# Projections of two tiles in one product: q, k and up from turned norms laid out by chunk, and the first norm two turns ahead

## The chip, the cores and the metric

The kernel runs on one core of one Trainium2 chip. The metric is device time in microseconds (us). The core has TensorE (PE; its weight loads are shown as PEld), VectorE (DVE), ScalarE (ACT), GpSimd (POOL) and SyncE (SP), which here only issues DMAs.

## The reference

The input is x with 8 sequences of 2048 rows of 256 numbers, in fp32. Two residual blocks follow each other:

```python
x = x + _layernorm(_L0_attn_ref(_layernorm(x)))
x = x + _layernorm(_L0_ffn_ref(_layernorm(x)))

# attention: q, k, v = h @ w.T ; sigma = elu + 1
a_mem = sigma_q @ memory                     # over norm = sigma_q @ memory_norm
A = (sq_i @ sk_i.T) * tril                   # chunks of 128 rows, state carried
out = (A @ v_i + sq_i @ S_kv) / den ; S_kv += sk_i.T @ v_i

# ffn: dense part and 1024 gated experts
dense = silu(h @ W_up.T) @ W_down.T          # W_up 1024 x 256
# experts: product keys, top 8 of 8 x 8 sums for each of 4 heads,
#   w = silu((h @ de) * softmax) over the chosen ones, then w @ ue
```

## The kernel before

The 16384 rows are cut into 128 tiles of 128 rows. Tile t belongs to sequence t % 8, so that neighbouring tiles belong to different sequences and the carried state is not in each other's way. Everything is a software pipeline written out by hand: in step s, each engine runs `body`, in which the name `t[k]` is the tile s - k, so the tile that is at stage k. There are 142 steps ("turns" below); each engine runs through its own list in order, and semaphores tie them together. Nothing is reordered by a scheduler: the order of the code is the order of each engine.

The weights stand in SBUF, turned so that a product for a tile has a chunk of weights as stationary operand or as moving operand. Each product over the 256 numbers of a row needs two chunks (`DC` = 2), and each fp32 product is two instructions in the trace. The helper `product` (L691) records nearly all of them.

What TensorE does for a tile, in its order within a turn: up (stage 10: 8 blocks of 128 of W_up, tile as moving operand, 128 columns each, into banks 1 and 2), q and k (stage 7, 4 blocks of 128 columns, into bank 1), v (stage 7), the experts' output `ue,gT` (stage 13), the router `route` (stage 9), sigma_k times sigma_q `sig` (stage 7), half of the experts' input `deT`, the state and memory products (stage 7), the masked product (L817), the second half of `deT`, the addition to the state (L835, stage 8), and the down product `wdownT` (stage 12). PSUM banks 1 and 2 are used by up, by q and k and by the state in turn, so ScalarE has to evict each half of up (`hT`, Silu, L892 and L947) before the next use.

The norms are turned (rows to columns) off TensorE: VectorE makes the norm (`xn1`, `xn2`, L1055), turns it in blocks of 32 x 32 (`xn1_blocks` L1088, `xn2_blocks` L1115), SP writes the blocks to a DRAM buffer (`xn1_way`, `xn2_way`), and reads them back with 8 small DMAs into `xn1T` or `xn2T` (`gather_chunks`, L437: 16 KB each, in pieces of 128 bytes). The experts' weights (`w_blocks` L1127, `w_way`, read back as `g_parts` with 4 DMAs, L430) and sigma_k (`sk_blocks`, `sk_way`, `sk_nat`) go the same way. GpSimd adds up the four heads' weights with two accumulating DMAs per tile, of 1 MB (L597) and of 512 KB (L558), on a queue of its own. All transfers share the core's 16 DMA engines.

First norm: x is loaded in the turn t (`t[0]`), its statistics are made at `t[3]`, the norm at `t[4]`, the turning and the gather at `t[5]`, and q and k are made at `t[7]`. Second norm: norm, turning and gather at `t[8]`, and first use by TensorE at `t[9]`, by `route`, some 10 us into the turn; up follows at `t[10]`. After the step 23 and up to step 120 (`steady`), a few waits that others imply are left out.

## Time and profile before

| | |
|---|---|
| median of 3 runs | 2848.42 us (2846.77 to 2849.49) |
| the profiled execution | 2852.01 us, span 2850.3 us |
| mean granted TensorE clock | 0.997 of full |
| busy: PE, PEld, DVE, ACT, POOL | 99%, 80%, 85%, 89%, 72% |
| chain that ended last | PE 90%, of it L691 84% |
| DMA engines' mean busy share | 7 tenths in most slices |
| GpSimd's queue, SP's queue | 37.6%, 34.2% of 16 engines' span |

The first row is what versions are compared by, the second belongs to the rows shown below. A busy share is the part of the span in which an engine ran an instruction. The chain is the one that ended last, followed back from the end to what released each step.

### The profile page before, as it was taken

How to read it: one execution, taken by the hardware profiler on the slowest of the kernel's cores; microseconds unless marked ns; L12 is line 12 of the kernel's file. 1: busy time of each engine (PE TensorE's matmuls, PEld its weight loads, DVE VectorE, ACT ScalarE, POOL GpSimd, SP SyncE). 2: the span in 40 equal slices, each digit the busy share in tenths (PEclk: the TensorE clock that was granted, in tenths of full speed). 3: DMA queues.
4: the chain of work that ended last, by engine and by line, in shares of the span. 5: the costliest groups of instructions: out<-in, count | busy, mean ns of one | idle time of the engine just before them, and what ended most of it. 6: DMA issues, size and time to landing. Idle time of an engine off the chain costs nothing.

```text
span 2850.3 us, 49057 instructions
## 1 busy us (share of the span) xinstructions
PE 2819.8 (99%) x14724; PEld 2272.4 (80%) x14724; DVE 2422.5 (85%) x6125; ACT 2525.8 (89%) x3618; POOL 2060.4 (72%) x2460
## 2 busy tenths in 40 slices
PE   8899999999999999999999999999999999999999
PEld 6678878878887788788788878887887788788877
DVE  5888888888888888888888888888888888888886
ACT  5898998999899989988998999899988989998997
POOL 3677777777777777777777777777776777777674
PEclk9999999999999999999999999999999999999999
DMA  4677777777777777777777777777777776777664
GB/s 117 140 170 166 167 173 175 162 167 177 171 165 174 168 167 168 171 170 168 169 172 173 165 169 172 170 165 174 173 163 165 175 175 163 169 175 169 153 153 121
DMA packets 592910, 471.71 MB, mean 165 GB/s; under 512 B 377732, under 2 KB 527365, under 8 KB 592645
## 3 DMA queue, kind: packets, MB, share of 16 engines
q0 software_dynamic: 52832, 199.77, 37.6%
q1 hardware_dynamic: 539812, 268.81, 34.2%
q8 instruction: 117, 1.92, 0.3%
q14 instruction: 149, 1.21, 0.1%
HBM read 137.37 MB, written 131.20 MB: 94 GB/s over the span
## 4 chain that ended last, share of the span: by engine, by line
PE 90%; SPq 2%; POOL 2%; ACT 2%; DMA 2%; DVE 1%; issue 1%; POOLq 0%; DVEq 0%; ACTq 0%
PE banks L691 84%; PE banks L835 3%; PE banks L817 2%; SPq L437 1%; SPq L430 1%; POOL sums L539 1%; DMA w_way<-w_blocks 1%; DMA wexp<-wexp 0%; DMA g_parts<-w_way 0%; DVE w_blocks L1127 0%; POOL rstd L525 0%; ACT prob L986 0%; DVE prob L1119 0%; ACT L1008 0%; POOL wexp L597 0%
## 5 line engine op out<-in xcount | busy, mean ns | idle before, releaser
L539 POOL TENSOR_TENSOR sums<-scores 128x1024 f32<-128x1024 f32 x512 | 1005.2, 2047 | 78.2 <-ACT scores L1025 78.2
L525 POOL TENSOR_TENSOR rstd<-var_eps,minus_half 128x1 f32<-128x1 f32 x512 | 508.5, 993 | 42.2 <-ACT y_sq L935 15.6
L691 PE MATMUL banks<-deT,xn2T 128*128 128x512 f32 x1024 | 484.3, 596 | 2.5 <-DVE picked L1074 2.1
L691 PEld LDWEIGHTS banks<-xn2T,wupT 128*128 128x128 f32 x4096 | 477.2, 192 | 9.3 <-DVE state L1181 2.9
L691 PE MATMUL banks<-xn2T,wupT 128*128 128x128 f32 x4096 | 478.2, 275 | 2.1 <-DVE state L1181 2.1
L691 PE MATMUL banks<-ue,gT 128*128 128x256 f32 x2048 | 463.0, 379 | 0.5 <-ACT gT L964 0.5
L691 PE MATMUL banks<-wdownT,hT 128*128 128x256 f32 x2048 | 462.8, 379 | 0.2 <-ACT y_sb L1021 0.2
L691 PEld LDWEIGHTS banks<-wdownT,hT 128*128 128x128 f32 x2048 | 389.0, 190 | 56.9 <-issue 3.0
L691 PEld LDWEIGHTS banks<-ue,gT 128*128 128x128 f32 x2048 | 388.7, 190 | 53.8 <-ACT gT L964 0.9
L577 POOL TENSOR_TENSOR wexp<-wexp,w_last 128x1 f32<-128x1 f32 x127 | 131.8, 1038 | 370.6 <-ACT z_last L1014 370.6
L691 PEld LDWEIGHTS banks<-deT,xn2T 128*128 128x128 f32 x1024 | 185.8, 192 | 135.8 <-issue 125.0
L553 POOL TENSOR_TENSOR cprob<-cmask,cdif 128x112 f32<-128x112 f32 x128 | 58.9, 460 | 273.9 <-DVE cmask L1208 273.9
L691 PE MATMUL banks<-route,xn2T 128*128 128x512 f32 x512 | 240.9, 593 | 1.5 <-ACT xn2T L882 0.8
L1074 DVE SCALAR_TENSOR_TENSOR picked<-sums,cand_best,banks 128x1024 f32<-128x1024 f32 x128 | 163.9, 1280 | 51.5 <-POOL sums L539 51.5
L1173 DVE SCALAR_TENSOR_TENSOR picked<-sums,cand_best,banks 128x1024 f32<-128x1024 f32 x128 | 163.9, 1281 | 47.6 <-PE banks L691 46.8
L1194 DVE SCALAR_TENSOR_TENSOR prob<-picked,rz,prob 128x1024 f32<-128x1024 f32 x128 | 166.2, 1299 | 36.3 <-ACT prob L939 34.2
L1082 DVE SCALAR_TENSOR_TENSOR prob<-picked,rz,prob 128x1024 f32<-128x1024 f32 x128 | 166.7, 1302 | 27.2 <-ACT prob L986 26.8
L947 ACT ACTIVATE hT<-banks 128x512 f32<-128x512 f32 x128 | 76.6, 598 | 125.4 <-PE banks L691 125.1
L1186 DVE SCALAR_TENSOR_TENSOR picked<-sums,cand_best,banks 128x1024 f32<-128x1024 f32 x128 | 163.4, 1276 | 12.8 <-POOL sums L539 12.7
L896 ACT ACTIVATE wexp<-prob 128x1024 f32<-128x1024 f32 x127 | 134.2, 1057 | 39.0 <-DVE w_blocks L1127 38.9
L961 ACT ACT_TABLE_LOAD x128 | 164.2, 1283 | 2.3
L947 ACT ACT_TABLE_LOAD x128 | 164.2, 1283 | 2.3
(162 smaller groups left out, 6658.7 us busy)
## 6 DMA issues: line engine op xcount, KB each, us to landing
wexp<-wexp POOLq DMA_DIRECT2D x127, 1024.0 KB, 9.1
wexp<-wexp POOLq DMA_DIRECT2D x127, 512.0 KB, 4.7
w_way<-w_blocks SPq DMA_DIRECT2D x127, 512.0 KB, 2.7
g_parts<-w_way SPq DMA_DIRECT2D x508, 128.0 KB, 7.5
xn_way<-xn_blocks SPq DMA_DIRECT2D x248, 128.0 KB, 1.8
x_in<-_attn_hidden_states_dram SPq DMA_DIRECT2D x128, 128.0 KB, 2.4
out_dram<-x_out SPq DMA_DIRECT2D x128, 128.0 KB, 1.8
xn1T<-xn_way SPq DMA_DIRECT2D x1000, 16.0 KB, 2.0
```

The lines of the kernel that those rows point to most:

```text
L525: return nc.gpsimd.tensor_tensor(rstd[:, n, m:m + 1], var_eps[:, n, m:m + 1], minus_half[:, :], ALU.pow)
L539: return nc.gpsimd.tensor_tensor(sums[:, k, :, :], scores[:, k, 0:XIN].unsqueeze(2).broadcast_to([P, XIN, NKEYS]), scores[:, HEADS + k, :] ...
L577: nc.gpsimd.tensor_tensor(weights(t[9])[:, 0, LAST_IN:], weights(t[9])[:, 0, LAST_IN:], w_last[:, t[9] % 2:t[9] % 2 + 1], ALU.add).then_in ...
L691: last = nc.tensor.matmul(out, lhs(c), rhs(c), start=(start and c == 0), stop=(stop and c == chunks - 1))
L896: nc.scalar.activation(weights(t[10])[:, 3, :], prob[:, 3, :], ACT.Silu).then_inc(s_head_3_weights_ready, 1)
L947: nc.scalar.activation(flat(hT[:, t[9] % 3, 4:8, :]), u_ps[1][:, :], ACT.Silu).then_inc(s_hidden_1_ready, 1)
L961: nc.scalar.activation(prob[:, 3, :], head(sums, 3), ACT.Exp, bias=neg_max[:, t[9] % 2, 3:4]).then_inc(s_head_3_prob_ready, 1)
L1074: nc.vector.scalar_tensor_tensor(picked[:, 0, :], head(sums, 2), best[:, 2, TOP - 1:TOP], down, ALU.is_ge, ALU.mult).then_inc(s_head_2_sel ...
L1082: nc.vector.scalar_tensor_tensor(prob[:, 2, :], picked[:, 0, :], rz[:, t[10] % 2, 2:3], prob[:, 2, :], ALU.mult, ALU.mult).then_inc(s_head ...
L1173: nc.vector.scalar_tensor_tensor(picked[:, 0, :], head(sums, 0), best[:, 0, TOP - 1:TOP], down, ALU.is_ge, ALU.mult).then_inc(s_head_0_sel ...
L1186: nc.vector.scalar_tensor_tensor(picked[:, 1, :], head(sums, 1), best[:, 1, TOP - 1:TOP], down, ALU.is_ge, ALU.mult).then_inc(s_head_1_sel ...
L1194: nc.vector.scalar_tensor_tensor(prob[:, 1, :], picked[:, 1, :], rz[:, t[9] % 2, 1:2], prob[:, 1, :], ALU.mult, ALU.mult).then_inc(s_head_ ...
```

## The change

Three things change, and one follows from them.

1. `xn1T` and `xn2T` hold four tiles instead of two and are laid out chunk by chunk, so that the same chunk of two neighbouring tiles is one run of 256 columns. From tile 12 on (`PAIRED`) q, k and up are made for two tiles in one product of 256 columns. In even turns of stage 7 k is made for tiles t and t + 1, in odd ones q for t + 1 and t + 2 (q of tiles 12 and 13 is made once extra, in bank 0). Up for the pair is made half in the even tile's turn (blocks 0 to 3), half in the odd one's (blocks 4 to 7), for tiles 12 to 125. `hT` gets a fourth slot and `sig` a third buffer. The last tiles' up stays as it was; the last turn of stage 7 makes neither q nor k.
2. Up in an even turn now reads the second norm of tile u + 1 too, which is at stage 9 in that turn. On SP the gather of `xn2T` moves ahead of `sk_way` and of the read of `g_parts`, right behind `w_way`.
3. q in an odd turn reads the first norm of tile t + 2. So load, statistics, norm and turning of the first norm move: the tiles 10 and 14 (`AHEAD`) are taken along in a turn with another tile, and behind them every tile is one and then two turns ahead (`ahead`). The gather of `xn1T` stands behind the load of x and the gather of `sk_nat`, last in SP's turn but for the store.
4. ScalarE's eviction of up (`hidden`) writes parts of two tiles' `hT`; `sigma` writes two tiles' q or two tiles' k.

```diff
+    PAIRED = 12
+    AHEAD = (10, 14)
+    TURNED = 4
...
-        xn1T = sb("xn1T", [P, 2, DC, P])
-        xn2T = sb("xn2T", [P, 2, DC, P])
+        xn1T = sb("xn1T", [P, DC, TURNED, P])
+        xn2T = sb("xn2T", [P, DC, TURNED, P])
...
-        sig = sb("sig", [P, 2, 2 * DC, P])
+        sig = sb("sig", [P, 3, DC, 2, P])
...
-        hT = sb("hT", [P, 3, IC, P])
+        hT = sb("hT", [P, 4, IC, P])
...
+        def ahead(t, stage):
+            for lead in range(len(AHEAD) + 1):
+                u = t[stage - lead]
+                if u is not None and u not in AHEAD and len([a for a in AHEAD if a < u]) == lead:
+                    return u
+            return None
...
+            def up(t, half):
+                if not paired_up(t):
...
+                else:
+                    first = t // 2 * 2 % TURNED
+                    for k in range(2):
+                        ic = 4 * (t % 2) + 2 * half + k
+                        last = product(two_tiles(u_ps[half])[:, k, :, :], DC, lambda c: wupT[:, c, ic * P:(ic + 1) * P],
+                                       lambda c: xn2T[:, c, first:first + 2, :])
+                return last
+
+            def two_tile_q_or_k(dst, w, t):
+                for ec in range(DC):
+                    last = product(two_tiles(dst)[:, ec, :, :], DC, lambda c: w[:, c, ec * P:(ec + 1) * P],
+                                   lambda c: xn1T[:, c, t % TURNED:t % TURNED + 2, :])
+                return last
...
+                    if paired_up(u) and u % 2 == 0:
+                        moved(pe, s_xn2_blocks_in, u + 1, BLOCKS * DC, LATE, EARLY)
...
+                    elif t[7] % 2 == 0:
+                        two_tile_q_or_k(qk_ps, wkT, t[7]).then_inc(s_qk_in_psum, 1)
+                    elif t[7] < TILES - 1:
+                        two_tile_q_or_k(qk_ps, wqT, t[7] + 1).then_inc(s_qk_in_psum, 1)
...
+                for lead, a in enumerate(AHEAD):
+                    if t[3 - lead] == a:
...
+                        xn1_made(a - 1)
+                        dve.wait_ge(s_xn1_ready, a)
+                    if t[4 - lead] == a:
+                        xn1_turned(a)
```

SP's queue, one steady turn of before, from the store of the output on. `xn_way` stands for both norms' buffers: the first row of it is the second norm's, the next the first norm's.

```order
L483 DMA out_dram<-x_out 128x256
L444 DMA xn_way<-xn_blocks 128x256
L448 DMA xn_way<-xn_blocks 128x256
L452 DMA w_way<-w_blocks 128x1024
L456 DMA sk_way<-sk_blocks 128x256
L430 DMA g_parts<-w_way 32x4x256 x4
L437 DMA xn2T<-xn_way 32x4x32 x8
L437 DMA xn1T<-xn_way 32x4x32 x8
L475 DMA x_in<-in_L_attn_hidden_states_dram 128x256
L430 DMA sk_nat<-sk_way 32x4x64 x4
L483 DMA out_dram<-x_out 128x256
```

The same stretch of the changed kernel:

```order
L535 DMA out_dram<-x_out 128x256
L494 DMA xn_way<-xn_blocks 128x256
L483 DMA xn_way<-xn_blocks 128x256
L502 DMA w_way<-w_blocks 128x1024
L477 DMA xn2T<-xn_way 32x4x32 x8
L511 DMA sk_way<-sk_blocks 128x256
L470 DMA g_parts<-w_way 32x4x256 x4
L520 DMA x_in<-in_L_attn_hidden_states_dram 128x256
L470 DMA sk_nat<-sk_way 32x4x64 x4
L477 DMA xn1T<-xn_way 32x4x32 x8
L535 DMA out_dram<-x_out 128x256
```

The 8 DMAs of `xn2T` now stand in front of `sk_way` and the 4 of `g_parts`; those of `xn1T` stand behind `x_in` and `sk_nat`.

TensorE, one steady turn of before from up on, with what each row waits for:

```order
L691 MATMUL banks<-xn2T,wupT 128x128 [waits state_ready]
L691 MATMUL banks<-xn2T,wupT 128x128 x15
L691 MATMUL banks<-xn1T,wqT 128x128 [waits hidden_1_ready,xn1_blocks_in_1]
L691 MATMUL banks<-xn1T,wqT 128x128 x3
L691 MATMUL banks<-xn1T,wkT 128x128 x4
L691 MATMUL banks<-wvo,xn1T 128x256 x2
L691 MATMUL banks<-ue,gT 128x256 [waits expert_weights_T_ready]
L691 MATMUL banks<-ue,gT 128x256 x7
L691 MATMUL banks<-route,xn2T 128x512 [waits xn2_blocks_in_1]
```

The changed kernel, a turn in which the tile of up is even (q for two tiles):

```order
L747 MATMUL banks<-xn2T,wupT 128x256 [waits hidden_1_ready,state_ready,xn2_blocks_in_1]
L747 MATMUL banks<-xn2T,wupT 128x256 x3
L747 MATMUL banks<-xn2T,wupT 128x256 [waits hidden_0_ready]
L747 MATMUL banks<-xn2T,wupT 128x256 x3
L747 MATMUL banks<-xn1T,wqT 128x256 [waits hidden_1_ready,xn1_blocks_in_1,xn1_blocks_in_0]
L747 MATMUL banks<-xn1T,wqT 128x256 x3
L747 MATMUL banks<-wvo,xn1T 128x256 x2
L747 MATMUL banks<-ue,gT 128x256 [waits expert_weights_T_ready]
L747 MATMUL banks<-ue,gT 128x256 x7
```

And the turn ahead of it, with an odd tile at up (k for two tiles):

```order
L747 MATMUL banks<-xn2T,wupT 128x256 [waits hidden_1_ready,state_ready]
L747 MATMUL banks<-xn2T,wupT 128x256 x3
L747 MATMUL banks<-xn2T,wupT 128x256 [waits hidden_0_ready]
L747 MATMUL banks<-xn2T,wupT 128x256 x3
L747 MATMUL banks<-xn1T,wkT 128x256 [waits hidden_1_ready]
L747 MATMUL banks<-xn1T,wkT 128x256 x3
```

In place of 16 products of 128 columns for up and 8 for q and k stand 8 and 4 of 256 columns. In the even turn the very first product of up waits for `xn2_blocks_in_1`, the gather of tile u + 1's second norm, for which `route` waits too, but later in the same turn; the first product of an odd turn waits for no gather.

## Rows read from the trace of the kernel before

**Rows 1.** The page, part 1: busy time and share of the span of each engine.

```profile
PE 2819.8 (99%) x14724; PEld 2272.4 (80%) x14724; DVE 2422.5 (85%) x6125; ACT 2525.8 (89%) x3618; POOL 2060.4 (72%) x2460
```

**Rows 2.** Who waited for whom, TensorE, whole run: us in total, times, longest.

```profile
PE banks L817 <- DVE at L1153: 9.1, 5, 3.8
...
PE banks L691 <- DVE state L1181: 2.1, 2, 1.3
```

**Rows 3.** Timeline of TensorE, one steady turn: start us, us, engine, line, operation, tiles.

```profile
1411.66 3.73 PE L691 MATMUL banks<-xn2T,wupT 128*128 128x128 f32 x32
1415.23 1.06 PE L691 MATMUL banks<-xn1T,wqT 128*128 128x128 f32 x8
...
1417.01 1.03 PE L691 MATMUL banks<-wvo,xn1T 128*128 128x256 f32 x4
1417.88 3.62 PE L691 MATMUL banks<-ue,gT 128*128 128x256 f32 x16
1421.33 1.88 PE L691 MATMUL banks<-route,xn2T 128*128 128x512 f32 x4
...
1426.96 0.60 PE L817 MATMUL banks<-v_one,at 128*128 128x258 f32 x2
...
1433.43 3.73 PE L691 MATMUL banks<-xn2T,wupT 128*128 128x128 f32 x32
```

**Rows 4.** Groups of instructions by form, TensorE: busy us, mean ns.

```profile
L691 PE MATMUL banks<-xn2T,wupT 128*128 128x128 f32 x4096 | 478.2, 275 | 2.1 <-DVE state L1181 2.1
```

**Rows 5.** Timeline of ACT, DVE and POOL in the same turn; idle time before in brackets.

```profile
1417.21 0.60 ACT L975 ACTIVATE rqk<-banks 128x512 f32<-128x512 f32 x1 [0.51 <-PE banks L691]
...
1419.51 1.29 DVE L1082 SCALAR_TENSOR_TENSOR prob<-picked,rz,prob 128x1024 f32<-128x1024 f32 x1 [0.24 <-ACT prob L986]
...
1423.61 1.24 DVE L1127 STREAM_TRANSPOSE w_blocks<-wexp 128x1024 f32<-128x1024 f32 x1
...
1425.99 0.41 DVE L1144 BATCH_NORM_STATS2 stats<-x_in 128x6 f32<-128x256 f32 x1
...
1426.37 0.28 DVE L1153 TENSOR_TENSOR at<-banks,causal 128x128 f32<-128x128 f32 x1
...
1427.64 1.22 POOL L597 DMA_DIRECT2D wexp<-wexp  x1
1427.66 0.16 DVE L1156 TENSOR_SCALAR dens<-banks 128x2 f32<-128x2 f32 x1 [1.01 <-PE banks L817]
```

**Rows 6.** Timeline of SP's DMA issues around that turn: start us, us for all.

```profile
1421.53 1.80 SPq L430 DMA_DIRECT2D sk_nat<-sk_way  x4
...
1424.87 0.40 SPq L452 DMA_DIRECT2D w_way<-w_blocks  x1
1425.31 0.45 SPq L456 DMA_DIRECT2D sk_way<-sk_blocks  x1
1428.29 2.67 SPq L430 DMA_DIRECT2D g_parts<-w_way  x4
1431.00 7.46 SPq L437 DMA_DIRECT2D xn2T<-xn_way  x8
1438.51 4.73 SPq L437 DMA_DIRECT2D xn1T<-xn_way  x8
```

**Rows 7.** DMA view, issues at 1439.4, 1439.9, 1428.2, 1428.6: median us to landing.

```profile
xn1T<-xn_way SPq DMA_DIRECT2D x2, 16.0 KB, 1.8
...
xn1T<-xn_way SPq DMA_DIRECT2D x1, 16.0 KB, 4.0
...
g_parts<-w_way SPq DMA_DIRECT2D x1, 128.0 KB, 3.1
...
g_parts<-w_way SPq DMA_DIRECT2D x2, 128.0 KB, 4.7
```

**Rows 8.** DMA view, GpSimd's queue in 1429.4 to 1429.9, and 1440.5 to 1441.

```profile
q0 software_dynamic: 2, 0.01, 8.2%
...
q0 software_dynamic: 22, 0.09, 90.0%
```

More of the change, by code:

```diff
@@ L331, in pipeline, with sig_k, sig_q, q_buffer @@
                      STAGES + SLOTS <= step < KEPT)
+        def sig_k(t, c):
+            return sig[:, 0, c, t % 2, :]
+        def sig_q(t, c):
+            return sig[:, q_buffer(t), c, t % 2, :]
+        def q_buffer(t):
+            return 1 if t < PAIRED else 1 + ((t - PAIRED) // 2 + 1) % 2
+        def pair_of(t):
+            return t // 2 * 2 % 4
+        def ahead(t, stage):
[4 more added lines that the diff above has]
+            return None
+        def up_done(step):
+            return step - 9
+        def hidden_at(t):
+            return t // 2 * 2 + 2 if paired_up(t) else t + 1
+        def paired_up(t):
+            return PAIRED <= t < LATE
         def y_bank(t):
@@ L452, in body @@
                         sp.dma_start(w_way[t[11] % 2, :, :], w_blocks[:, :]).then_inc(s_expert_weights_blocks_out[t[11] % 2], 16)
+                if t[8] is not None:
+                    if EARLY <= t[8] < LATE:
+                        moved(sp, s_xn2_blocks_out, t[8], 1, LATE, EARLY)
+                        wait(sp, s_up_0_in_psum, t[8] - 2)
+                        gather_chunks(xn2T[:, :, t[8] % TURNED, :], xn2_way[t[8] % 2, :, :], s_xn2_blocks_in[t[8] % 2])
                 if t[7] is not None:
@@ L480, in body @@
                         gather(sk_nat[:, t[7] % 2, :, :].rearrange('p (i t) c -> p i (t c)', t=BLOCK), sk_way[t[7] % 2, :, :], s_sk_blocks_in[t[7] % 2])
+                if x is not None:
+                    if x - 1 in AHEAD:
+                        xn1_in(x - 1)
+                    if x >= EARLY:
+                        xn1_in(x)
+                if x is not None and x + 1 in AHEAD:
+                    xn1_out(x + 1)
                 if t[13] is not None:
@@ new lines, in up @@
+            def up(t, half):
+                if not paired_up(t):
+                    for k in range(4):
+                        ic = 4 * half + k
+                        last = product(u_ps[half][:, k * P:(k + 1) * P], DC, lambda c: wupT[:, c, ic * P:(ic + 1) * P],
+                                       lambda c: xn2T[:, c, t % TURNED, :])
+                else:
[5 more added lines that the diff above has]
+                return last
@@ L718, in body @@
                         turn_wdown(0, 0)
-                    if t[10] == TILES - 3:
+                    if u == TILES - 3:
                         turn_xn('xn2', xn2, s_xn2_ready, LATE)
-                    if t[10] == TILES - 2:
+                    if u == TILES - 2:
                         turn_xn('xn2', xn2, s_xn2_ready, LATE + 1)
-                    wait(pe, s_state_ready, t[10] + 2, KEPT)
-                    for k in range(4):
-                        ic = 4 + k
-                        last = product(u_ps[1][:, k * P:(k + 1) * P], DC, lambda c: wupT[:, c, ic * P:(ic + 1) * P],
-                                       lambda c: xn2T[:, t[10] % 2, c, :])
@@ L728, in body @@
-                    last.then_inc(s_up_1_in_psum, 1)
-                    if not steady:
-                        wait(pe, s_hidden_0_ready, t[10])
-                    for k in range(4):
-                        ic = k
-                        last = product(u_ps[0][:, k * P:(k + 1) * P], DC, lambda c: wupT[:, c, ic * P:(ic + 1) * P],
-                                       lambda c: xn2T[:, t[10] % 2, c, :])
-                    last.then_inc(s_up_0_in_psum, 1)
+                    if paired_up(u) and u % 2 == 0:
+                        moved(pe, s_xn2_blocks_in, u + 1, BLOCKS * DC, LATE, EARLY)
@@ L1174, in body @@
                                                    ALU.is_ge, ALU.mult).then_inc(s_head_0_selected, 1)
-                if t[3] is not None:
-                    dve.wait_ge(s_x_stats, t[3] + 1)
-                    nc.vector.bn_aggr(mv[:, LN_X, t[3] % 2, :], stats[:, LN_X, t[3] % 2, :]).then_inc(s_x_moments, 1)
+                x = ahead(t, 3)
+                if x is not None and x - 1 not in AHEAD:
+                    x_moments(x)
                 if t[8] is not None:
```

266 lines of the change are left out of this document (172 added, 94 removed).

## The prediction

> **What bounds the kernel now.** I read the page's busy shares first. TensorE is busy 99% of the span, no other engine over 89% [rows 1]. Then its waits: over the whole run it waited 9.1 us for the causal mask in five places and 2.1 us for the state, and nothing else of size [rows 2]; the same view cut to the first 400 us gives the same sums, so they belong to the filling of the pipeline. So I went to its timeline. A steady turn begins with up at 1411.66, and the next begins at 1433.43: 21.77 us. Each group starts before the modelled end of the one ahead, and none has an idle time in brackets [rows 3]. Some 115 of the 142 turns look like this. As long as nothing makes TensorE wait, the time is the sum of the pitches of its instructions, and a change is worth what it takes out of that sum.
>
> The timeline of the others says how near they are. VectorE waits 1.01 us at L1156 for L817, which is the round trip over TensorE and back, and otherwise a little here and there: 0.24 us ahead of L1082 for ScalarE [rows 5].
>
> **The saving.** The trace has products of both widths with the same 128 x 128 weights, so the price needs no model. Up takes 1415.23 - 1411.66 = 3.57 us for 32 instructions of 128 columns, 0.112 each; q and k take 1417.01 - 1415.23 = 1.78 us for 16. The 16 instructions of 256 columns of `ue,gT` take 1421.33 - 1417.88 = 3.45 us, 0.2156 each [rows 3]. The trace's 4096 up instructions are 32 for each of 128 tiles, so a tile really has 32 [rows 4]. Two of 128 cost 0.223, one of 256 costs 0.216.
> - Up as 16 of 256: 16 x 0.2156 = 3.45, saves 0.12 us per tile, on the 114 tiles 12 to 125: 13.7 us.
> - q and k as 8 of 256 per turn: 1.725 instead of 1.78, saves 0.055 us, on 116 turns: 6.4 us.
> - Together 20.1 us, or 0.175 us of each turn.
>
> By the Trainium skill (TensorE: Matmul & The Clock Gate, Back-to-back issue gap) a product costs its columns and some 2.5 ns. By that, one of 256 in place of two of 128 saves 2.5 ns, and 24 of these per tile make 0.06 us, about 7 us in all. The rows disagree with it: they show 7.6 ns for a pair, and I go by the rows.
>
> **Can the others follow a turn of 21.6 us?** Two chains matter. From the end of q or k over relu, exp, sigma and VectorE's queue to the mask and L817, both ends move together, since nothing of TensorE's between q/k and L817 changes. The mask ends at 1426.65, L817 begins at 1426.96 [rows 3, 5], so a room of at most 0.31 us stays as it is. From L817 back to itself one turn later, VectorE does its whole list; it idles 0.24 us ahead of L1082, because ScalarE is late there, and ScalarE itself waits 0.51 us at L975 for q and k [rows 5]. The turn shrinks by 0.175, which is less than 0.24. So the loop just follows, with 0.06 us left. The evictions and sigma write the same number of elements in another order; I cost that at nothing, covered by the 0.51 us and by these rooms. If a rearranged write takes over 0.1 us more, it shows at L817 in every turn.
>
> **The moved gather.** An even turn's up now needs the second norm of the tile behind it. Until now that was read by `route`, 9.7 us into the turn (1421.33 against 1411.66). So SP sends it earlier. Before, its 8 DMAs are issued from 1431.00 to 1438.46, because they stand behind `g_parts`, which stands behind the landing of `w_way` [rows 6]; that would be 5 us too late for an up at 1433.43. Now they follow `w_way`. `w_blocks` is ready at 1424.85 [rows 5], `w_way` is issued at 1424.87, the next DMA at 1425.31, and four DMAs of `sk_nat` take 1.80 us, 0.46 each [rows 6]. So the eighth is issued at 1425.31 + 7 x 0.46 = 1428.5, at most 1428.65 with 0.475 each. With a landing 1.8 us later [rows 7] it is there at 1430.4, some 2.9 us ahead of up. That is cost nothing, if it lands undisturbed.
>
> What could disturb it is GpSimd's accumulation of 1 MB, issued at 1427.64 (L597). The trace shows what such a one does to small DMAs. Around the smaller one of this queue (L558, issued at 1439.08), the two `xn1T` DMAs near 1439.4 took 1.8 us, the next, half a microsecond later, took 4.0 [rows 7], and GpSimd's packets began in 1440.5 to 1441 (22 of them) [rows 8]. So one issued up to some 1.0 us ahead of these packets passes, a later one doesn't. After the 1 MB issue only 2 such packets ran until 1429.9 [rows 8]. That puts the limit near 1428.8, and the eighth DMA at 1428.5 to 1428.65 just ahead of it. `g_parts` DMAs, eight times larger, show both sides: issued at 1428.3 one landed after 3.1 us, the next had 6.3 (the two have a median of 4.7) [rows 7].
>
> Everything on SP behind the gather has cover. `sk_way` and `g_parts` go out some 3 to 4 us later than now, and are wanted a good half turn later; the gather of `xn1T`, last in the turn, has until q two turns on. SP no longer waits for the landing of `w_way` with 12 DMAs behind it (1425.31 + 0.45 to 1428.29, a gap of 2.5 us [rows 6]), so its turn gets shorter. `x_in` is now read one turn after its load instead of three; a turn is 21.6 us.
>
> **Once-only costs.** Tiles 10 and 14 put a second first norm into two turns: five short VectorE instructions, the statistics being 0.41 [rows 5]; I estimate 1.6 us together, less the 0.24 of room, 1.3 us twice. In the turn of tile 12 TensorE makes q one time extra (1.7 us), which the last turn, having neither q nor k, gives back; ScalarE does two further passes of 0.60 [rows 5] and VectorE a further sigma, about 1.9 us on the way to L817. Together 4.5, I take 5 us; bounds 0 (hidden in waits of the filling) and 10.
>
> **Sum.** -20 + 5 = -15 us. The profiled execution took 2852.0 us, so the changed one should take 2837; the median of before is 3.6 lower than that execution, so the median forecast is 2848.4 - 15 = 2833.4. The forecast's own range is 2828 (no once-only cost) to 2839.
>
> **Rivals.**
> - *The eighth DMA is caught* (19%). It is the slower case. The margin is 0.15 to 0.3 us of issue time, and the trace doesn't show how fast SP issues while `w_way` is moving: if the DMAs behind it are slowed by a single 0.3 us, the last one falls behind the limit. Then it lands like the second `g_parts` did, 6.3 us after 1428.65, at 1434.95, where up wants it at 1433.26: a wait of 1.7 us every second turn, 57 x 1.7 = 97 us, so 2848 - 15 + 97 = 2930. If it happens in one even turn out of four, it costs 24 us: 2858. It decides from one turn in six on (16 us). For it speaks how sharp the step from 1.8 to 4.0 is; against it, that the 1 MB issue starts its packets over 2 us after the issue, and that all of it (w_blocks, w_way, GpSimd's issue) hangs on the same VectorE instruction, so that its distances repeat. The Trainium skill (DMA: Bandwidth & Descriptors, Queues, rings and completion order) says that an engine goes round between its queues packet by packet, so a small DMA behind large packets is slowed, not blocked; the 4.0 us agrees.
> - *The loop of VectorE, ScalarE and GpSimd doesn't follow* (9%). Room 0.06 us; if the split patterns of sigma and of the evictions cost 0.1 to 0.2 us more, half of the gain or all of it goes: 2840 to 2851.
> - *The change doesn't do what it says* (4%): a product of 256 columns over two tiles has a pitch between the 0.2156 of `ue,gT` and the 0.223 of two narrow ones, because its operand or its target is read and written in another pattern. Halfway it saves 10 us, less 5: 2843. By the skill's gap it would be 7 less 5, 2846.
>
> **Chances.** Forecast 68%. A measurement of this kernel tells about 0.2% (5.7 us) from no change. Faster: the forecast and the better half of the small losses, 71%. Within 0.2%: 11%. Slower: 18%. The range of 2827 to 2860 holds the forecast, both small rivals and the mild form of the first; its full form stays outside.
>
> **What would show it.** Turns of 21.60 us in TensorE's timeline, with up in 3.45 us and q or k in 1.73; no row of TensorE waiting for `xn2T<-xn_way`. The first rival would show as just that wait, near 1.7 us, in even turns alone, with VectorE's wait for L817 grown. The second would show as L817 waiting for the mask in every turn, and ScalarE's `hT` above 0.60. The last `xn2T` issue should stand about 0.9 us behind GpSimd's 1 MB issue; I am wrong if it stands over 1.2 behind.

## The result, and the profile after

The changed kernel takes 3103.99 us (median of 4 runs, 3096.10 to 3104.31) against 2848.95 for the kernel before (4 runs, 2846.77 to 2852.42): 1.089 times the time, 95% interval 1.0878 to 1.0903. The forecast of 2833.4 was wrong in direction. The profiled execution has a span of 3102.3 us, with a mean granted clock of 0.965. Of all the runs below one is left out, the fourth of experiment 7, which took 4229 us at a granted clock of 0.654 where its three others agree within 4 us.

The page of the changed kernel, parts 1, 4 and 5 (in part 5 the time behind the bar is busy time and mean, then the idle time ahead and what ended it):

```profile
PE 2909.2 (94%) x11972; PEld 2241.8 (72%) x11972; DVE 2428.0 (78%) x6125; ACT 2525.9 (81%) x3618; POOL 2046.7 (66%) x2460
...
PE 41%; DMA 20%; SPq 14%; DVE 9%; issue 6%; ACT 6%; POOL 4%; DVEq 0%; ACTq 0%; POOLq 0%
...
L747 PE MATMUL banks<-xn2T,wupT 128*128 128x256 f32 (+1 forms) x2272 | 561.7, 409 | 158.5 <-DMA xn2T<-xn_way 156.4
```

Against [rows 1], ScalarE has as much work as before and VectorE 5.5 us more; TensorE has 2752 instructions fewer and yet 89 us more busy time. So two things happened: TensorE stood idle, and it ran slower. The chain of waits was 90% TensorE before; now a third of it is a DMA and the queue that issues it. TensorE's waits, whole run, to be read against [rows 2]:

```profile
PE banks L747 <- DMA xn2T<-xn_way: 156.4, 55, 4.8
PE banks L906 <- DVE at L1291: 14.1, 9, 3.8
```

Fifty-five waits for the gather of the second norm, which is the number of pairs but for two. The timeline of TensorE over two turns, against [rows 3]:

```profile
1505.08 3.62 PE L747 MATMUL banks<-xn2T,wupT 128*128 128x256 f32 x16
1508.53 1.89 PE L747 MATMUL banks<-xn1T,wkT 128*128 128x256 f32 x8
...
1523.22 3.62 PE L747 MATMUL banks<-wdownT,hT 128*128 128x256 f32 x16
1529.53 5.31 PE L747 MATMUL banks<-xn2T,wupT 128*128 128x256 f32 x16 [2.69 <-DMA xn2T<-xn_way]
1534.67 1.89 PE L747 MATMUL banks<-xn1T,wqT 128*128 128x256 f32 x8
...
1552.81 3.62 PE L747 MATMUL banks<-xn2T,wupT 128*128 128x256 f32 x16
```

The up of an odd turn, the second half of a pair, begins at 1505.08 and the next group at 1508.53, so it takes 3.45 us, as forecast. The up of the even turn behind it, the first half of the next pair, begins after a wait of 2.69 us and takes 1534.67 - 1529.53 = 5.14 us for the same 16 instructions. The same stretches by window (busy us of each engine, then granted clock, DMA share, GB/s) give the reason:

```profile
1505.08:1508.53 3.45, 3.45 (x17) 3.04 (x16) 3.20 (x5) 2.42 (x3) 0.70 (x2) 1.00 0.99 160
1526.07:1529.53 3.46, 0.78 (x5) 0.35 (x3) 2.77 (x3) 1.50 (x2) 1.94 (x2) 0.98 1.00 163
1529.53:1534.67 5.14, 5.14 (x16) 4.28 (x17) 3.74 (x8) 1.51 (x2) 4.59 (x6) 0.68 0.90 194
1534.67:1540.71 6.04, 6.04 (x29) 5.32 (x28) 2.51 (x4) 5.57 (x8) 0.00 (x0) 1.00 0.42 73
```

The granted clock over these products is 0.68 of full, a mean of its two levels (2.4 and 1.2 GHz) with two thirds of the 5.14 us at the lower; before it fell, TensorE had stood still for 2.69 us. In the stretch of the wait the DMA engines are busy all the time. The wait itself costs a little more than its bracket says: the bracket counts from the modelled end of the down product (1523.22 + 3.62), while the next group would have begun 3.45 us behind its start, at 1526.67, so up comes 2.86 us late. From up to up the one turn measures 24.45 us (1505.08 to 1529.53) and the one behind it 23.28; against twice 21.60 (experiment 6) two turns lose 2.86 + 1.69 = 4.5 us.

Why the gather is late stands in SP's issues and GpSimd's of that turn, against [rows 6] and the last rows of [rows 5]:

```profile
1518.12 0.32 SPq L502 DMA_DIRECT2D w_way<-w_blocks  x1
1518.60 4.04 SPq L477 DMA_DIRECT2D xn2T<-xn_way  x8
1522.68 0.84 SPq L511 DMA_DIRECT2D sk_way<-sk_blocks  x1
...
1520.89 1.23 POOL L653 DMA_DIRECT2D wexp<-wexp  x1
```

The eighth goes out at 1522.2, 1.3 us behind the 1 MB accumulation. The DMA view of windows that hold the accumulation and the sixth, the seventh, and then only the eighth (median us to landing, of one DMA each), against [rows 7]:

```profile
wexp<-wexp POOLq DMA_DIRECT2D x1, 1024.0 KB, 8.4
xn2T<-xn_way SPq DMA_DIRECT2D x1, 16.0 KB, 1.7
...
xn2T<-xn_way SPq DMA_DIRECT2D x1, 16.0 KB, 4.6
...
xn2T<-xn_way SPq DMA_DIRECT2D x1, 16.0 KB, 7.3
```

The sixth, issued 0.4 us behind the accumulation's issue, lands in 1.7 us. The seventh, at 0.85, takes 4.6. The eighth, at 1.3, takes 7.3: it lands at 1529.5, and the accumulation itself at 1520.89 + 8.4 = 1529.3. The seventh landed at 1521.73 + 4.6 = 1526.3, in the middle of it. What runs on the DMA engines meanwhile tells why. GpSimd's queue is q0 and SP's q1 (packets, MB, share of the 16 engines); first the changed kernel from 1523 to 1525.75, then the kernel before from 1441 to 1443, behind its smaller accumulation:

```profile
DMA packets 256, 0.54 MB, mean 197 GB/s; under 512 B 128, under 2 KB 128, under 8 KB 256
q0 software_dynamic: 128, 0.52, 106.3%
q1 hardware_dynamic: 128, 0.02, 7.9%
...
q0 software_dynamic: 102, 0.42, 110.2%
```

A 16 KB gather in pieces of 128 bytes is 128 packets, the 1 MB in pieces of 4 KB is 256. In the first stretch they go one for one, 128 to 128, and GpSimd's fill the time. So a gather that begins in the accumulation advances one small packet for each large one: the seventh needs half of the accumulation, the eighth, behind it in SP's queue, the other half, which is why, by these counts, the eighth lands with it. The second stretch shows another picture: GpSimd's packets run and none of SP's, although SP issued a gather at 1439.9 that lands 4.0 us later [rows 7]. Why the one lets SP's packets through and the other doesn't, no run here shows.

### The profile page after: what moved, and what is told of

Its sections match the earlier page's. It is cut to its first block, busy times and chain, and to the rows that moved or that the text cites. A ratio compares the mean times of both kernels' runs of the same rounds, so it can differ in the third digit from the quotient of the medians.

```text
span 3102.3 us, 44218 instructions
## 1 busy us (share of the span) xinstructions
PE 2909.2 (94%) x11972; PEld 2241.8 (72%) x11972; DVE 2428.0 (78%) x6125; ACT 2525.9 (81%) x3618; POOL 2046.7 (66%) x2460
## 4 chain that ended last, share of the span: by engine, by line
PE 41%; DMA 20%; SPq 14%; DVE 9%; issue 6%; ACT 6%; POOL 4%; DVEq 0%; ACTq 0%; POOLq 0%
PE banks L747 38%; DMA xn2T<-xn_way 13%; SPq L477 12%; DMA sk_way<-sk_blocks 5%; POOL sums L591 2%; DVE prob L1257 2%; DVE w_blocks L1265 2%; ACT prob L1088 2%; DMA xn_way<-xn_blocks 2%; SPq L470 1%; ACT rqk L1077 1%; PE banks L924 1%; DVE x_out L1247 1%; DVE xn_blocks L1180 1%; DVE xn L1160 1%
## 5 line engine op out<-in xcount | busy, mean ns | idle before, releaser
L747 PE MATMUL banks<-xn2T,wupT 128*128 128x256 f32 (+1 forms) x2272 | 561.7, 409 | 158.5 <-DMA xn2T<-xn_way 156.4
L747 PEld LDWEIGHTS banks<-xn2T,wupT 128*128 128x128 f32 x2272 | 459.0, 220 | 252.3 <-DMA xn2T<-xn_way 178.5
L629 POOL TENSOR_TENSOR wexp<-wexp,w_last 128x1 f32<-128x1 f32 x127 | 124.1, 977 | 615.8 <-ACT z_last L1116 615.8
L986 ACT ACTIVATE hT<-banks 128x512 f32<-128x512 f32 x228 | 137.0, 601 | 331.0 <-PE banks L747 330.5
L1157 DVE SCALAR_TENSOR_TENSOR sig<-banks,rqk 128x512 f32<-128x512 f32 x115 | 79.0, 687 | 234.4 <-ACT banks L1079 234.4
L1324 DVE SCALAR_TENSOR_TENSOR picked<-sums,cand_best,banks 128x1024 f32<-128x1024 f32 x128 | 163.4, 1277 | 12.7 <-POOL sums L591 12.6
```

What stands on the lines that cost most here:

```text
L629: nc.gpsimd.tensor_tensor(weights(t[9])[:, 0, LAST_IN:], weights(t[9])[:, 0, LAST_IN:], w_last[:, t[9] % 2:t[9] % 2 + 1], ALU.add).then_in ...
L747: last = nc.tensor.matmul(out, lhs(c), rhs(c), start=(start and c == 0), stop=(stop and c == chunks - 1))
L986: nc.scalar.activation(hT[:, pair_of(t):pair_of(t) + 2, ic:ic + 2, :].rearrange("p t i n -> p i t n"), two_tiles(u_ps[half]), ACT.Silu).th ...
L1324: nc.vector.scalar_tensor_tensor(picked[:, 1, :], head(sums, 1), best[:, 1, TOP - 1:TOP], down, ALU.is_ge, ALU.mult).then_inc(s_head_1_sel ...
```

## The experiments

Theory A: all that the steady turns lose is that TensorE wants a gather whose last transfers land only with the 1 MB accumulation; the clock falls because of that wait. Rivals: the accumulation harms in another way; the pairing itself makes TensorE or a consumer slower; SP's order is at fault in general. Each kernel was timed beside the kernel before on the same chip, and its ratio is to that: 2848.70 us for experiments 1 to 4, 2849.05 for 5 to 8, 2850.23 for 9, 2848.57 for 10 and 11, 2849.52 for 12.

**1. Up for one tile.** q and k stay paired, SP's order stays that of the change.

```diff
         def paired_up(t):
-            return PAIRED <= t < LATE
+            return False
```

> Up is made for one tile at a time again, as before the change; q and k stay in pairs, and the order of SP and the first norm's lead stay as changed. Theory A (the loss is up's wait for the next tile's second norm, and what the clock does behind it): no such wait, turns of 21.72 us, and with the once-only costs of the filling 2845 to 2858 us. Theory B (the loss lies in the pairing of q and k, the first norm's lead or the fuller SP queue): the time stays over 3000 us. Theory C (both share it): in between.

2854.71 us, ratio 1.0019 (1.0009 to 1.0028), turns of 21.72 us. The same late gather harms nobody when up doesn't read it, so neither q and k nor SP's order cost anything in the steady turns. It is not faster than before, though its turns are 0.05 us shorter: its first turns hold something, see experiment 5.

**2. The 1 MB accumulation 1.2 us later.** In GpSimd's list it stands behind `cdif` and `neg_max`, ahead of `key_sums(1)`.

```diff
+                if t[8] is not None:
+                    pool.wait_ge(s_best_ready, t[8] + 1)
+                    nc.gpsimd.tensor_tensor(cdif[:, :, :], ...
+                    nc.gpsimd.tensor_tensor(neg_max[:, t[8] % 2, :], ...
                         pool.dma_start(wexp[:, 1::2, :], wexp[:, 0::2, :], accum_op=ALU.add)
                 if t[8] is not None:
-                    pool.wait_ge(s_best_ready, t[8] + 1)
-                    nc.gpsimd.tensor_tensor(cdif[:, :, :], ...
-                    nc.gpsimd.tensor_tensor(neg_max[:, t[8] % 2, :], ...
                     key_sums(1).then_inc(s_head_1_sums_ready, 1)
```

> GpSimd issues the 1 MB accumulation behind cdif and neg_max instead of ahead of them, some 1.3 to 1.9 us later; all else is as changed. Theory A1 (the last gathers of the second norm are caught behind this accumulation's packets): the eighth gather is issued under 0.3 us ahead of or behind the accumulation, lands in 1.8 us, the wait is gone, and the whole is 2835 to 2848 us. Theory A2 (the gather is late by its own issue behind the 512 KB write, whatever GpSimd does): the wait of 2.7 us every second turn stays, and the time is 3090 to 3110.

2934.05 us, ratio 1.0290 (1.0273 to 1.0307), between the two ranges expected. Its TensorE waits:

```profile
PE banks L907 <- DVE at L1292: 72.4, 122, 3.2
PE banks L748 <- DMA xn2T<-xn_way: 5.7, 1, 5.7
```

The eighth now goes out 0.1 us ahead of the accumulation and lands in 1.7 us; 54 of 55 waits are gone with the clock's fall (0.996). Every turn pays for it in another place: GpSimd's 1.2 us of issue delay the sums that VectorE waits for (130.9 us in its waits, 12.6 in the change), and with them the mask, 0.6 us in each of 122 turns of 22.28. So a shift of the accumulation of 1.2 us cures the gather, and GpSimd has no such 1.2 us to give there.

**3. The gather ahead of the write of `w_blocks`.**

```diff
-                sp.dma_start(w_way[...], w_blocks[:, :])
                 gather_chunks(xn2T[...], xn2_way[...], ...)
+                sp.dma_start(w_way[...], w_blocks[:, :])
```

> SP issues the eight gathers of the second norm ahead of the 512 KB write of w_blocks instead of behind it; GpSimd is as changed. Both A1 and A2 expect the wait to go, since the eighth gather is issued 1.2 us sooner against the accumulation and nothing of SP's stands before it: 2835 to 2850 us. If the write, now issued near the accumulation, comes too late for what reads it, TensorE would wait for gT instead, with more than 2860 us.

3085.98 us, ratio 1.0840 (1.0806 to 1.0874): only 18 us less than the change, against both theories. TensorE still waits for the gather, 147.4 us in 47 places.

```profile
1522.58 3.64 SPq L477 DMA_DIRECT2D xn2T<-xn_way  x8
1526.27 0.43 SPq L507 DMA_DIRECT2D w_way<-w_blocks  x1
1529.13 4.46 SPq L470 DMA_DIRECT2D g_parts<-w_way  x4
...
1525.77 1.23 POOL L653 DMA_DIRECT2D wexp<-wexp  x1
```

In the turn shown the eighth goes out at 1525.8, together with the accumulation, and the issue of all eight takes 3.64 us, not 4.04: the slow second issue of the change is that behind the write of 512 KB. But `w_way` now moves while the accumulation does, `g_parts` follows late, SP's turn overruns, and in the other turn of the pair the gather starts so late that it is caught after all. The order alone isn't the cure.

**4. Fill the wait.** Seven products that nobody reads, ahead of up in even turns.

```diff
+                    if u % 2 == 0 and 16 <= u < TILES - 8:
+                        for k in range(7):
+                            nc.tensor.matmul(bank[0][:, 0:D], wqT[:, 0, 0:P], wvo[:, 0, :], start=True, stop=True)
```

> Seven products of 256 columns whose result nobody reads (14 instructions, 3.0 us) stand ahead of up in the even turns from tile 16 to 118, where TensorE waits 2.7 us as changed. Nothing else changes. Theory K (behind the wait the granted clock is at its lower level for a while, which costs 1.7 to 1.9 us more): the clock stays up, up takes 3.45 us in every turn, and the 52 pairs become 1.6 us shorter each: 3010 to 3030 us. Theory L (up is slow after the wait for another reason, such as its operands): no gain, 3100 to 3120 us.

3039.39 us, ratio 1.0662 (1.0645 to 1.0679), clock 0.994:

```profile
1522.44 3.62 PE L747 MATMUL banks<-xn2T,wupT 128*128 128x256 f32 x16
...
1544.03 3.19 PE L803 MATMUL banks<-wvo,wqT 128*128 128x256 f32 x14
1547.05 3.62 PE L747 MATMUL banks<-xn2T,wupT 128*128 128x256 f32 x16
```

TensorE does 3.0 us of useless work and the kernel is 65 us faster than the change. The turn is 24.61 us, and up behind the filler takes 3.46. So the slow up was the clock's answer to the wait and not something of the paired products. The time misses the expected 3010 to 3030 by 9 us: in 21 turns the gather came later than the filler lasted (25.3 us in all). Behind 16 of these waits, up to 0.99 us long, up took 3.56; behind the other five, of 2.56 to 4.34 us, it took 5.24 once more.

**5. The write of `xn1` sooner.** In the change's first turns VectorE shows two waits that the kernel before doesn't have:

```profile
180.86 0.45 DVE L1180 STREAM_TRANSPOSE xn_blocks<-xn 128x256 f32<-128x256 f32 x1 [3.05 <-DMA xn_way<-xn_blocks]
...
252.78 0.45 DVE L1180 STREAM_TRANSPOSE xn_blocks<-xn 128x256 f32<-128x256 f32 x1 [4.37 <-DMA xn_way<-xn_blocks]
```

These are the turns after tiles 10 and 14 were taken along: SP writes their `xn1_blocks` out last, behind 8 or 16 gathers, and VectorE may not turn the next norm into the buffer until then.

```diff
+                if x is not None and x + 1 in AHEAD:
+                    xn1_out(x + 1)
                 if x is not None:
                     if x - 1 in AHEAD:
                         xn1_in(x - 1)
                     if x >= EARLY:
                         xn1_in(x)
-                if x is not None and x + 1 in AHEAD:
-                    xn1_out(x + 1)
```

> The changed kernel, in which SP writes out the turned first norm of tiles 10 and 14 ahead of that turn's gathers of the first norm instead of behind them. Theory: the once-only costs of the filling (two turns of 4.7 and 6 us over the rest) come from VectorE waiting 3 to 4 us for that write before it may turn the next norm; with it sooner by 8 to 16 small DMAs the two waits go and the whole gets 8 to 12 us shorter: 3092 to 3096 us. Rival (they come from the extra VectorE work itself): at most 2 us shorter.

3094.10 us, ratio 1.0861 (1.0845 to 1.0878), 10 us less than the change; the two turns went from 26.53 and 28.21 to 21.78 us each. The next kernels all have this edit. It doesn't always cure both: in the traces of experiments 8 and 12 VectorE still waits 2.4 and 2.3 us for the same write in the second of the two turns, which takes 25.8 and 25.7 us.

**6. A small accumulation.** The same two DMAs at the same place, the large one over 128 of its 1024 columns, so 256 pieces of 512 bytes and not of 4 KB. The other columns are left out of the sum, and the output is not the reference's.

```diff
-                        pool.dma_start(wexp[:, 1::2, :], wexp[:, 0::2, :], accum_op=ALU.add)
+                        pool.dma_start(wexp[:, 1::2, 0:P], wexp[:, 0::2, 0:P], accum_op=ALU.add)
```

> As e5_write_out_sooner, and GpSimd's large accumulation covers 128 of 1024 columns, so 128 KB in place of 1 MB, with the same number of pieces; the other columns are left out of the sum, so the output is not the reference's. SP's order is as changed. Theory A1 (the last gathers are caught behind the 1 MB's packets): no wait, turns of 21.6 us throughout, 2830 to 2836 us. Theory A2 (late by SP's own queue): the wait stays and the time is over 3050 us. This run also tells what the pairing would be worth without the wait: 20 us by the sum of the prediction.

2831.18 us, ratio 0.9941 (0.9926 to 0.9956). The gather goes out as late as in the change (the eighth 1.32 us behind in the median), lands after 2.1 us where it was 7.3, TensorE doesn't wait for it, and the turns are 21.60 us:

```profile
1514.37 3.62 PE L747 MATMUL banks<-xn2T,wupT 128*128 128x256 f32 x16
1535.97 3.62 PE L747 MATMUL banks<-xn2T,wupT 128*128 128x256 f32 x16
...
1530.17 1.22 POOL L653 DMA_DIRECT2D wexp<-wexp  x1
```

That is Theory A's clearest case: with the transfer short, the turns are the predicted ones, from 21.77 to 21.60. It is still an accumulation with as many pieces, so what holds the gather back is their size, and not their number or that they accumulate. (The total stands near the forecast of 2833.4 with the 10 us of experiment 5 taken out; with them it would be some 2841.)

**7. All gathers first.** SP's order: gather of xn2, `w_way`, `sk_way`, load of x, gather of xn1, `sk_nat`, `g_parts` last.

> As e5_write_out_sooner, and SP's turn is put in this order: gather of the second norm, write of w_blocks, write of sigma_k, load of x, gather of the first norm, gather of sigma_k, read of g_parts. So nothing behind the gather waits for the write of w_blocks until the end of SP's turn, which was what upset the order in e3_gather_first. If the eighth gather is then issued no later than 0.3 us behind the 1 MB accumulation in every turn, the wait is gone: 2832 to 2842 us, faster than both kernels. If g_parts comes too late, TensorE waits for gT and it is 2850 to 3000 us.

3024.73 us (3 runs), ratio 1.0615 (1.0594 to 1.0636), waits of 114.8 us in 50 places, and neither of the expected causes. In many turns the write of `xn2_way`, on which the gather hangs, now falls together with `g_parts`, at times with the end of the 512 KB accumulation too, and takes 2.4 to 4 us instead of 1.8; that brings the eighth to 1 us and more behind the 1 MB again. In turns where it was issued with it, it landed in 1.7.

**8. Up for one tile, with edit 5.**

> As e5_write_out_sooner, with up for one tile at a time: the pairs of q and k alone. Turns of 21.72 us as in e1_up_single, that is 6 us off the sum of before, and with the once-only cost cut from 14 to some 3 us: 2843 to 2847 us, or 8 to 12 us under e1_up_single. If the once-only cost does not come from the late write, 2853 to 2856 us.

2848.93 us, ratio 0.9996 (0.9987 to 1.0006), turns of 21.72: pairing q and k alone is worth nothing that can be measured in the whole time. It is 2 us over the range expected; the wait of 2.4 us named under 5 is there. The step from here to experiments 6 and 12 is up's: 18 us in the one, which also moves less data, 8 in the other, some 11 without its extra products. By the turns it is 21.72 to 21.60, on 114 tiles the 13.7 us that were forecast.

**9. Everything on the gather's way sooner.** VectorE turns xn2 right behind making it (0.9 us sooner), SP issues the gather ahead of `w_way`, and the output's store moves from the end of SP's turn to behind `w_way`.

> The change with the write of xn1 sooner in the two early turns (as in e5_write_out_sooner), and three moves that bring xn2's gather ahead of GpSimd's 1 MB accumulation: VectorE turns xn2 right behind making it, ahead of xn1, of the turned state and of x_out (some 0.9 us sooner); SyncE issues xn2's gather ahead of the write of w_blocks; the output's store stands behind that write and no more at the end of SyncE's turn. The products stay paired and the accumulation stays where it is. If what the change loses is only that the pair's second gather lands with the 1 MB accumulation (the theory), its eighth transfer now goes out some 0.75 us ahead of that accumulation's issue and lands within 2 us, no turn waits for xn2T, the granted clock stays at 1.00 and the turns are the 21.60 us of e6_small_big_add: 2831 to 2838 us, with the whole computation. Rival: a transfer issued next to GpSimd's two large ones is caught whichever it is. Then the write of w_blocks or the gather of g_parts lands with the 1 MB, TensorE waits for the expert weights or SyncE's turn overruns and the gather slides back behind the accumulation: 2950 us and more, as in e3_gather_first and e7_all_gathers_first.

2962.95 us, ratio 1.0389 (1.0351 to 1.0427). In half of the turns (55 of 103 in the steady part) it works: the eighth goes out 0.4 us ahead of the accumulation or with it, lands in 1.8 us, and turns measure 21.71. But the 512 KB of `w_way` took the place of the gather. SP's issues in a turn with a late start:

```profile
1533.67 0.43 SPq L494 DMA_DIRECT2D xn_way<-xn_blocks  x1
...
1536.06 3.65 SPq L477 DMA_DIRECT2D xn2T<-xn_way  x8
1539.75 0.43 SPq L507 DMA_DIRECT2D w_way<-w_blocks  x1
...
1546.32 1.98 SPq L470 DMA_DIRECT2D g_parts<-w_way  x3
```

and from SP's waits of the whole run:

```profile
SPq L316 <- DMA w_way<-w_blocks: 245.3, 126, 7.2
```

`w_way` landed in 2.8 us in the turn before and in 6.5 here (GpSimd's 1 MB went out at 1538.77), SP waited for it ahead of `g_parts`, and each such turn starts the next one late, until a gather is caught: 22 waits, 69.1 us. So the rival stated with this kernel holds: whichever transfer of SP stands next to the accumulation is caught.

**10 and 11. The accumulation at the end of GpSimd's turn**, behind `key_sums(1)`, some 3.5 us later; once with the order of experiment 5, once with that of 9.

```diff
-                        pool.dma_start(wexp[:, 1::2, :], wexp[:, 0::2, :], accum_op=ALU.add)
...
                     key_sums(1).then_inc(s_head_1_sums_ready, 1)
+                if t[9] is not None:
+                    if t[9] < TILES - 1:
+                        pool.dma_start(wexp[:, 1::2, :], wexp[:, 0::2, :], accum_op=ALU.add)
```

> e5_write_out_sooner with GpSimd's 1 MB accumulation issued at the end of its turn, behind the second of the two 128x1024 sums of keys that stand together there, some 3.5 us later; unlike e2_big_add_later it stands ahead of none of the sums that this turn needs, but ahead of the next turn's first. Theory (the gather is caught only because its last transfers go out behind that accumulation): all eight go out ahead of it and land in about 2 us, no turn waits for xn2T, and if the 1.2 us of issue are covered by GpSimd's idle 2.04 us ahead of the next turn's cprob, the turns are 21.60 us: 2829 to 2838 us. Rivals: the issue delays the next turn's first sum and each turn grows by up to the 0.68 us of e2_big_add_later: 2915 to 2935 us. Or the gather of g_parts, which goes out just there, is caught in its place and TensorE or ScalarE waits for the expert weights: 2950 us and more.

> The two moves together: the order of VectorE and SyncE of e9_norm_turned_sooner and the 1 MB accumulation at the end of GpSimd's turn of e10_add_at_the_end. Now xn2's gather, the write of w_blocks and the first transfers of g_parts all go out ahead of the accumulation. If e9 lost only by the write of w_blocks and what stands behind it landing with the accumulation (they took 5.9, 5.1 and 4.5 us there and pushed SyncE's next turns), none of them is caught here and the turns are even: 2829 to 2840 us. If GpSimd's issue costs the next turn's sum time, both kernels of this pair show it, about 0.1 to 0.7 us a turn: 2845 to 2935 us. Rival: SyncE's turn overruns for another reason, and hiccups of 2 to 4 us stay in every other to fifth pair as in e9: 2900 us and more.

2960.14 us, ratio 1.0389 (1.0373 to 1.0404), and 3010.38 us, ratio 1.0570 (1.0547 to 1.0594). Neither has a row of TensorE waiting for the gather `xn2T<-xn_way`. Instead, in the first of the two:

```profile
PE banks L908 <- DVE at L1293: 108.6, 122, 3.8
```

In the second this wait is 149.6 us. The eighth lands in 1.7 us, and the turns are 22.3 to 23.6 us long in the first, mostly 22.5 to 23.9 in the second. GpSimd still idles 2.04 us ahead of `cprob` in each turn, so that time doesn't take up the issue. Besides, GpSimd now waits for the 1 MB to land before it can issue the 512 KB, in 70 turns of the first and 59 of the second. Both times lie above the ranges that were given for a cost of GpSimd's issue alone. The second is 50 us slower than the first, which the new order of VectorE and SP must cost; I have not taken that apart.

**12. The pair one turn later.** Now nothing is moved ahead of the accumulation; TensorE asks later. Both halves of a pair are made in the turns of the tiles 2m + 1 and 2m + 2.

```diff
+        def up_jobs(u):
+            pair = ('pair', (u - 1) // 2 * 2, (u - 1) % 2)
+            if u <= PAIRED:
+                return [(u, ('one', u, 0))]
+            if u < LATE:
+                return [(u, pair)]
+            if u == LATE:
+                return [(u, pair), (u + 1, ('one', u, 0))]
+            return [(u + 1, ('one', u, 0))]
...
-                    up(u, 1).then_inc(s_up_1_in_psum, 1)
-                    wait(pe, s_hidden_0_ready, u)
-                    up(u, 0).then_inc(s_up_0_in_psum, 1)
+                    for n, job in up_jobs(u):
+                        wait(pe, s_hidden_1_ready, n)
+                        up(job, 1).then_inc(s_up_1_in_psum, 1)
+                        wait(pe, s_hidden_0_ready, n)
+                        up(job, 0).then_inc(s_up_0_in_psum, 1)
```

ScalarE's `hidden` walks through the same jobs, and the counts that the down product and SP's gather wait for move by one.

> e5_write_out_sooner with the paired up products one turn later and nothing else moved: both halves of the pair 2m, 2m+1 are made in the turns of the tiles 2m+1 and 2m+2, not 2m and 2m+1, so that the second tile's gather has a whole turn more before TensorE reads it. The turn of tile 12 multiplies that tile alone once more (3.45 us, of no use to the result), and the turn of tile 126 has both the last half pair and its own tile. Theory (all that the change loses in its steady turns is that TensorE wants the caught gather at once): its transfers still land up to 9 us behind GpSimd's 1 MB accumulation, but nobody waits for them, the granted clock stays at 1.00, the turns are the 21.60 us of e6_small_big_add, and the time is its 2831 us with 3.5 us for the extra products: 2832 to 2840 us, ratio 0.994 to 0.997, with the whole computation. Rivals: the caught transfers also hold SyncE's queue back and the expert weights or the next write comes late (a wait of 1 to 3 us in many turns, 2880 us and more); or what reads the hidden values, 10 us behind the products that make them and not a turn later, now waits for ScalarE (up to 1 us a turn, 2890 us and more).

2841.09 us (6 runs, 2836.94 to 2842.97) against 2849.52 (10 runs): ratio 0.9970, interval 0.9957 to 0.9982, with the whole computation. This version is faster than both kernels, against the one before by 0.3%. Its TensorE waits and two turns:

```profile
PE banks L917 <- DVE at L1309: 13.2, 10, 3.8
```

```profile
1515.71 3.62 PE L758 MATMUL banks<-xn2T,wupT 128*128 128x256 f32 x16
1537.31 3.62 PE L758 MATMUL banks<-xn2T,wupT 128*128 128x256 f32 x16
```

The turns are 21.60 us, the clock 0.998, and TensorE has no wait for the gather `xn2T<-xn_way`. The gathers are as late as in the change: in the median over the turns the eighth goes out 1.32 us behind the accumulation and lands after 7.3. Being caught costs nothing when nobody asks. The median is 1 us above the range expected, which had counted the 3.5 us of extra products but not the wait of 2.3 us named under 5, whose turn is 4 us longer than in experiment 6.

## Why the prediction was wrong

**The saving was right.** It said 21.77 to 21.60, by 0.12 for up and 0.055 for q and k. Turns measured 21.72 with q and k paired and 21.60 with up too; up takes 3.45. The row of a 256-column product for other operands [rows 3] priced it exactly, and the gap of 2.5 ns of the Trainium skill (TensorE: Matmul & The Clock Gate, Back-to-back issue gap), counted once for each instruction as the prediction did, by which the saving would be a third, is not borne out.

**The loop follows**, as said: experiments 6 and 12 run at 21.60, with a wait in only a handful of the steady turns. Room estimated at 0.06 us was enough.

**The step that failed: "That is cost nothing, if it lands undisturbed"**, the moved gather's cost, with the eighth DMA at 0.9 to 1.0 us behind the 1 MB issue and a limit at 1.16. Both numbers were off, in the direction that hurts:
- The issue. I took 0.46 per DMA from `sk_nat` [rows 6]. The second issue behind the 512 KB write took 0.78 us, and `sk_way` was no example of it; the eighth stands at 1.3, over the 1.2 that I had named as the mark of being wrong. In experiment 3, without the write ahead, the eight take 3.64 instead of 4.04. The rival had said that a single slowing of 0.3 us would decide, and it was this one.
- The limit. In the trace of the change, over all its steady turns, a DMA of this gather that was issued up to 0.7 us behind the accumulation landed after 2.6 us at most, one issued from 0.8 us on after 4.6 us at least. So even at the forecast 0.9 the eighth would have been caught. My rule, that one issued 1.0 us ahead of the accumulation's first packets passes, held; but these come 1.8 us behind the issue in the change (median), not 2.2 as in the kernel before, whose [rows 8] I used. A calculation of margins of 0.15 to 0.3 us from another transfer's rows could not carry the 68% that I put on it.

Of the two the issue weighs more. By an estimate from these rows an eighth DMA at 0.9, alone in being caught, would land some 4.6 to 5.0 us later, 5.5 to 5.9 behind the accumulation's issue, and up begins 5.8 behind it (1526.67 against 1520.89): next to no wait. At 1.3, with the seventh caught ahead of it, it takes 7.3.

**The rival was named and underpriced.** It was to cost 97 us, and the loss against the forecast is 271. Its wait of 1.7 us used the 6.3 us of `g_parts` for landing. The measured parts, added up over the 55 waits from the starts of the groups in the trace: up begins 165 us late in all (156.4 by the brackets), and, missing from the prediction altogether, it then takes 97 us longer than 3.45 us each, 1.8 us behind every wait, at the lower clock. With 9 us more of once-only costs than forecast that is 271 us, the whole loss.

The rule of queues served packet by packet, of the Trainium skill (DMA: Bandwidth & Descriptors, Queues, rings and completion order), is what the trace shows under the 1 MB, 128 packets to 128. I had set it beside the 4.0 us as agreeing, and there it doesn't: in that stretch GpSimd's packets ran alone. What the prediction lacked was the price that the rule gives: 128 packets of a gather against 4 KB each, and the same again for the one behind it. Experiment 6 bears this out, with pieces of 512 bytes. Whether a transfer that only copies would do the same, no run here shows: all of GpSimd's transfers in these kernels accumulate.

**Once-only costs.** Forecast 5 us, bounds 0 and 10; measured some 14, of which 10 are the two waits of VectorE for the write of `xn1`. I had counted instructions, and not that SP's write stood last in its turn with a buffer hanging on it.

## What to carry to other kernels

When a read is moved to an earlier turn, look at what else is on the DMA engines between its issue and its need, and price being caught by packets, not by bytes and not at the excess of the nearest one seen: here 128 small pieces went against 128 large ones, and each further small DMA that is caught adds its own. If the margin is a few tenths of a microsecond, take it as gone. A wait put on a TensorE that is otherwise never idle costs itself and then the lower clock, here 1.8 us for 2.8, so filling or removing it is worth more than its row says. And look first at letting the consumer ask a turn later, which cost 3.5 us once here: the six attempts to change what goes out first (experiments 2, 3, 7, 9, 10 and 11) all stayed at 2934 us or more, with the same wait or another in its place.

## What the runs showed of the hardware

- A 16 KB DMA of SP issued 0.4 us behind GpSimd's 1 MB accumulation lands in 1.7 us, one at 0.85 in 4.6, one at 1.3 in 7.3, together with the accumulation. While the 1 MB ran, SP's packets of 128 bytes went one for one with its packets of 4 KB (128 and 128 in 2.75 us). With pieces of 512 bytes, experiment 6, the last one lands in 2.1. `w_way`, 512 KB, goes from 2.8 to 6.5 us beside the 1 MB (experiment 9).
- The granted clock fell behind each of the 55 waits of the changed kernel, 2.5 to 4.8 us long: up took 5.0 to 6.3 us instead of 3.45. With seven products in the wait it didn't fall, where the gather then came within 1 us. It doesn't follow from the wait's length alone: in experiment 9 one of 2.83 us was followed by an up of 3.56, and one of 1.06 as well:

```profile
1200.11 3.72 PE L747 MATMUL banks<-xn2T,wupT 128*128 128x256 f32 x16 [2.83 <-DMA xn2T<-xn_way]
1203.67 1.89 PE L747 MATMUL banks<-xn1T,wqT 128*128 128x256 f32 x8
...
1567.76 3.72 PE L747 MATMUL banks<-xn2T,wupT 128*128 128x256 f32 x16 [1.06 <-DMA xn2T<-xn_way]
```

- SP's issue of a 16 KB gather takes 0.43 us and the second one behind a 512 KB write 0.78.
- GpSimd's issue of its 1 MB accumulation takes 1.2 us, and its next sum comes later by that; placed ahead of a sum that is wanted it costs TensorE 0.6 us of waiting a turn (experiment 2), at the end of the turn 0.9 to 1.2 (experiments 10 and 11).
